# Two transformer layers on one core: the token shift as transfers within SBUF, scores in four banks, and a new order on all engines

## What is computed

```python
def _layer(x, wqkv, qs, ksc, wo, lg, lb, w1, b1, w2, b2):
    h = shift_token(x)                       # the upper half of the channels comes from the token before
    q, k, v = jnp.split(h @ wqkv, 3, axis=-1)
    ...
    q, k = rotary_xpos(l2norm(q) * qs, l2norm(k) * ksc)
    o = local_attention(q, k, v)             # 8 heads of 64, two windows of 128
    x = x + o @ wo
    h = shift_token(x)
    h = (h - mu) / jnp.sqrt(var + 1e-05) * lg + lb
    a, g = jnp.split(h @ w1 + b1, 2, axis=-1)
    return x + (a * gelu(g)) @ w2 + b2
...
x = x + xattn(layernorm(x), ctx)
x = x + layer1(layer0(layernorm(x)))
```

## Time and profile before

| | |
|---|---|
| median of 3 runs (lowest, highest) | 1527.01 us (1526.02, 1528.28) |
| profiled execution | 1526.93 us |
| its span, first to last instruction | 1524.4 us |
| mean granted TensorE clock | 0.981 of 2.4 GHz |
| busy: PE, PE weight load | 1441.3 us (95%), 1277.3 us (84%) |
| busy: DVE (VectorE), ACT (ScalarE), POOL (GpSimd) | 1130.8 us (74%), 938.4 us (62%), 747.1 us (49%) |
| chain that ended last, by engine | PE 75%, DVE 12%, issue 5%, ACT 4%, POOL 2% |

### The profile page before, as it was taken

How to read it: one execution, slowest core, us unless ns; L and a number is a source line. 1 busy time by engine, 2 the same in 40 slices (tenths; PEclk the granted TensorE clock), 3 DMA queues, 4 the chain that set the end, 5 groups by cost and what they waited for, 6 DMA issues and landing times.

```text
span 1524.4 us, 33616 instructions
## 1 busy us (share of the span) xinstructions
PE 1441.3 (95%) x11808; PEld 1277.3 (84%) x11808; DVE 1130.8 (74%) x3102; ACT 938.4 (62%) x2670; POOL 747.1 (49%) x570
## 2 busy tenths in 40 slices
PE   4999999867999999999999899999999999999997
PEld 3888888746889889998888788888888888888886
DVE  3766666456888878887878778878888887888864
ACT  2766666435666666666666667666666666666661
POOL 1121121044666666666555555555565555566642
PEclk8999999889999999999999999999999999999998
DMA  6311111200000000000000110010010001011000
GB/s 196 103 57 48 50 53 44 84 29 15 24 24 24 25 25 23 23 23 24 30 31 24 45 41 24 17 47 31 31 32 31 30 30 30 30 34 40 24 24 26
DMA packets 40843, 58.88 MB, mean 39 GB/s; under 512 B 6540, under 2 KB 22448, under 8 KB 40752
## 3 DMA queue, kind: packets, MB, share of 16 engines
q1 hardware_dynamic: 40752, 57.69, 11.7%
HBM read 38.06 MB, written 16.78 MB: 36 GB/s over the span
## 4 chain that ended last, share of the span: by engine, by line
PE 75%; DVE 12%; issue 5%; ACT 4%; POOL 2%; DMA 1%; SPq 1%; DVEq 0%; POOLq 0%; ACTq 0%
PE pb L511 33%; PE pb L788 7%; PE pb L733 6%; PE pb L802 6%; PE pb L764 5%; PE pb L748 4%; PE pb L826 4%; PE pb L572 2%; PE pb L560 2%; PE pb L610 2%; PE pb L614 2%; DVE p_t L1383 2%; DVE r_cos L1350 2%; DVE p_t L1369 1%; DVE n_sq L1336 1%
## 5 line engine op out<-in xcount | busy, mean ns | idle before, releaser
L1559 POOL TENSOR_TENSOR n_inv<-n_cl,half_neg 128x16 f32<-128x16 f32 x64 | 211.4, 3303 | 190.8 <-DVE n_cl L1341 187.3
L1058 ACT ACTIVATE p_t<-p_t,s_nm 128x128 f32<-128x128 f32 (+1 forms) x512 | 227.2, 448 | 19.5 <-DVE s_nm L1369 18.8
L511 PE MATMUL pb<-h_hi,w_hi 128*128 128x256 f32 x704 | 208.8, 297 | 5.3 <-DVE h_lo L1332 3.3
L511 PE MATMUL pb<-h_lo,w_hi 128*128 128x256 f32 x704 | 199.7, 284 | 0.0
L511 PE MATMUL pb<-h_hi,w_lo 128*128 128x256 f32 x704 | 199.7, 284 | 0.0
L1564 POOL TENSOR_TENSOR r_cos<-r_cos,r_sin 128x1024 f32<-128x1024 f32 x64 | 154.7, 2417 | 88.8 <-DVE r_sin L1356 88.8
L1016 ACT ACTIVATE qk_sq<-pb 128x512 f32<-128x512 f32 x128 | 72.5, 592 | 183.6 <-PE pb L511 183.6
L1049 ACT ACTIVATE pt_t<-pb 128x512 f32<-128x512 f32 x192 | 114.5, 597 | 107.0 <-PE pb L748 106.6
L1369 DVE CUSTOM_DVE_ANT_0 p_t<-pb,mask_t 128x128 f32<-128x128 f32 (+1 forms) x512 | 152.0, 353 | 28.5 <-PE pb L733 27.3
L511 PE MATMUL pb<-wqkv_hi,xt_hi 128*128 128x512 f32 x384 | 166.9, 435 | 5.8 <-DVE r_sin L1356 4.9
L1586 POOL TENSOR_TENSOR hg_lo<-hg,hg_hi 128x256 fp32r<-128x256 f32 x192 | 139.6, 748 | 55.4 <-DVE hg_hi L1400 55.4
(11 more groups left out here) (137 smaller groups left out, 4083.1 us busy)
## 6 DMA issues: line engine op xcount, KB each, us to landing
y_state<-x SPq DMA_DIRECT2D x32, 256.0 KB, 2.0
x_cur<-y_state SPq DMA_DIRECT2D x32, 256.0 KB, 2.7
x_res<-y_state SPq DMA_DIRECT2D x32, 256.0 KB, 2.8
x_in<-x SPq DMA_DIRECT2D x16, 256.0 KB, 2.9
x_state<-x SPq DMA_DIRECT2D x16, 256.0 KB, 2.0
x_orig<-x_state SPq DMA_DIRECT2D x16, 256.0 KB, 2.8
out<-x SPq DMA_DIRECT2D x16, 256.0 KB, 2.2
raw_a<-wqkv SPq DMA_DIRECT2D x2, 1536.0 KB, 8.5
```

The costliest lines, as they stand in the source:

```text
L511: mm = pe.matmul(dst, s, m, start=(n == 0 and k == 0), stop=(n == len(pairs) - 1 and k == 2))
L1058: e = nc.scalar.activation(pu, pu, ACT.Exp, bias=s_nm[:, j, k:k + 1], scale=-1.0, accum_out=s_sum[:, j, k:k + 1])
L1559: nc.gpsimd.tensor_tensor(n_inv[:, t], n_cl[:, t], half_neg[:], ALU.pow).then_inc(pool_inv, 1)
```

## The change

- The shift of x1: TensorE's three products and VectorE's copy are gone; SyncE issues three transfers from SBUF to SBUF (112 rows, 15 rows, one row), and stats_h waits for them. They stand at the head of SyncE's iteration, behind the load of x for the next item; the tail copies of item d come behind them and behind the loads of x_res and x_orig.
- Scores pair 1 goes to banks 5 and 6, so it needs no maxima of pair 0; it waits for x1 (bank 6 has the output product before).
- Turned probabilities have six places. The rotated sine parts have one place in place of two, so rotate waits for the add_parts before it.
- Second bias: in layer 1 it is two rows of the last chunk's weights against rows of ones; the kept rows then are x1 plus the sum of the first phase, and the add L1412 is gone. Layer 0 keeps bias and kept rows as before.
- hidden 5 stands last on TensorE; x_hi waits for the last projection.

The new orders. TensorE: scores 0 and 1, project 0,0, feed 0, project 0,1, feed 1 and 2, project 0,2, scores 2, feed 3, turn_p 0, feed 4 and 5, turn_h, project 1,0 and 1,1, turn_next, turn_p 1, project 1,2, turn_p 2, hidden 0, turn_p 3, hidden 1, turn_p 4, hidden 2, turn_p 5, weigh 0 to 2, hidden 3 and 4, out_product 0, turn_qk 0 to 3, out_product 1, hidden 5.

VectorE: maxes 0, gate_hi 3 of item d, maxes 1 to 3, stats_h, gate_hi 4 and 5, inverse_sums 0, norm_probs 0, inverse_sums 1, rotate 0, inverse_sums 2, norm_h, maxes 4, squares 0, clamp 0, maxes 5, norm_probs 1, inverse_sums 3, second_residual, split_h_hi, norm_probs 2, split_h_lo, norm_probs 3, inverse_sums 4, rotate 1, norm_probs 4, squares 1, gate 0, inverse_sums 5, norm_probs 5, clamp 1, gate 1 and 2, out_lo 0, x_lo, gate 3, gate_hi 0 and 1, gate 4, out_lo 1, gate_hi 2, residual, gate 5.

GpSimd: deviation, gate_lo 3 to 5 of item d, add_parts 0, inverse_norms 0, add_parts 1, inverse_norms 1, norm_qk 0 and 1, kept_rows, gate_lo 0 to 2. ScalarE: the exponentials of units 0 and 1 ahead of the first squares, copies of turned probabilities between the gelus, gelu 5 last.

```diff
+SHIFT_PIECES = [(0, 112), (112, 15)]
...
-        S_BANK = [3, 4, 3, 4, 3, 4]
+        S_BANK = [3, 4, 5, 6, 3, 4]
...
+            def shift_down(c):
+                for first, rows in SHIFT_PIECES:
+                    sp.dma_start(x1[first + 1:first + 1 + rows, :, 1], x1[first:first + rows, :, 2]).then_inc(shift_load, 16)
+                sp.dma_start(x1[0:1, 1, 1], x1[P - 1:P, 0, 2]).then_inc(shift_load, 16)
...
+                if c is not None:
+                    sp.wait_ge(dve_x1, at(c, 1, 1))
+                    shift_down(c)
+                    if b is not None:
+                        sp.dma_start(x_res[:], one(y_dram, seq_of(b, layer))).then_inc(res_load, 16)
...
-            def shift_down(c):
-                pe.wait_ge(dve_x1, at(c, 1, 1))
-                pe.matmul(pb[:, 6, 0:P], down_f, x1[:, 0, 2], start=True, stop=True)
-                pe.matmul(pb[:, 6, P:2 * P], down_f, x1[:, 1, 2], start=True, stop=False)
-                pe.matmul(pb[:, 6, P:2 * P], carry_f, x1[:, 0, 2], start=False, stop=True).then_inc(pe_down, 1)
...
+                elif j == 1:
+                    if c is not None:
+                        pe.wait_ge(dve_x1, at(c, 1, 1))
                 else:
-                    pe.wait_ge(dve_max, at(b, UNITS, 2 * j))
+                    pe.wait_ge(dve_max, at(b, UNITS, 2))
...
-            def copy_shifted(c):
-                dve.wait_ge(pe_down, at(c, 1, 1))
-                nc.vector.tensor_copy(x1[:, :, 1], pb[:, 6, 0:2 * P].rearrange("p (t n) -> p t n", t=NT)).then_inc(dve_down, 1)
-
             def stats_h(c):
-                dve.wait_ge(dve_down, at(c, 1, 1))
+                dve.wait_ge(shift_load, at(c, 48, 48))
...
-                if layer_of(d, layer) == LAYERS - 1:
-                    dve.wait_ge(dve_x2, at(d, 1, 1))
-                    dve.wait_ge(orig_load, at(plus(d, -SEQS), 16, 16))
-                    nc.vector.tensor_tensor(x2[:, par], x2[:, par], x_orig[:], ALU.add).then_inc(dve_out, 1)
...
-            def residual_bias(c, d, layer):
-                ly = layer_of(c, layer)
+            def kept_rows(c, d, layer):
                 pool.wait_ge(dve_x1, at(c, 1, 1))
...
+                if layer_of(c, layer) == LAYERS - 1:
+                    pool.wait_ge(orig_load, at(plus(c, -SEQS), 16, 16))
+                    more = x_orig[:].rearrange("p t (c n) -> p t c n", c=KC)
```

More of the change, by code:

```diff
@@ L473, in run_l @@
                     tail_lo(d)
[L474 to L481, removed]
-                    if layer_of(d, layer) == LAYERS - 1:
[L483 to L490, removed]
+                    sp.wait_ge(dve_x2, at(d, 1, 1))
+                    dst = out_rows if layer_of(d, layer) == LAYERS - 1 else y_dram
+                    sp.dma_start(one(dst, seq_of(d, layer)), x2[:, 1 - par]).then_inc(x2_store[1 - par], 16)
             def between(g):
@@ L498, in _ @@
             l_iterations(sp, run_l, between)
-            sp.wait_ge(x2_store, 16 * ITEMS)
+            for u in range(2):
+                sp.wait_ge(x2_store[u], 8 * ITEMS)
         @block.tensor
@@ L714, in hidden, with scores @@
                 mm.then_inc(pe_w1, 1)
-            def scores(a, b, j):
+            def scores(a, b, c, j):
                 if j == 0:
@@ L832, in run_l @@
                 if b is not None:
[L833 to L837, removed]
+                    scores(a, b, c, 0)
+                    scores(a, b, c, 1)
                 if a is not None:
@@ L875, in run_l @@
                 if b is not None:
+                    turn_p(a, b, d, 3)
+                if c is not None:
+                    hidden(a, b, c, 1)
+                if b is not None:
                     turn_p(a, b, d, 4)
                 if c is not None:
-                    hidden(a, b, c, 1)
                     hidden(a, b, c, 2)
@@ L888, in run_l @@
                     out_product(b, 0)
-                if c is not None:
-                    hidden(a, b, c, 5)
                 if a is not None:
@@ L897, in run_l @@
                     out_product(b, 1)
+                if c is not None:
+                    hidden(a, b, c, 5)
             def between(g):
@@ L1137, in run_l @@
                     next_weights(g, 2)
+                if has_next(a):
+                    x_hi(plus(a, 1))
+                if b is not None:
+                    probs_copy(b, 5)
+                    out_hi(b, 0)
+                if c is not None:
                     gelu(c, 3, layer)
+                if b is not None:
+                    out_hi(b, 1)
+                if c is not None:
                     gelu(c, 4, layer)
-                    gelu(c, 5, layer)
                 if a is not None:
@@ L1145, in run_l @@
                     copy_qk(a, 3)
+                if c is not None:
+                    gelu(c, 5, layer)
             def between(g):
@@ L1475, in run_l @@
                 if c is not None:
-                    gate(c, 0, layer)
-                if b is not None:
-                    out_lo(b, 0)
-                if c is not None:
+                    gate(c, 3, layer)
                     gate_hi(c, 0)
@@ L1492, in run_l @@
                 if c is not None:
-                    gate(c, 5, layer)
-                    gate_hi(c, 3)
-                    gate_hi(c, 4)
-                    gate_hi(c, 5)
+                    gate_hi(c, 2)
                 if b is not None:
                     residual(b)
+                if c is not None:
+                    gate(c, 5, layer)
                 if isinstance(g, int) and g == SEQS - 1:
@@ L1637 @@
     w2 = rows_padded(L0_ffn_w2, FC * P)
-    for copy in (1, 2):
-        w2[:, HID + (copy - 1) * TAIL:HID + copy * TAIL] = w2[:, HID - TAIL:HID]
+    tail = w2[:, HID - TAIL:HID]
+    w2[:, HID:HID + TAIL] = tail
+    w2[:, HID + TAIL + 1:HID + 2 * TAIL + 1] = tail
+    for row in (HID + TAIL, HID + 2 * TAIL + 1):
+        w2[LAYERS - 1, row] = np.asarray(L0_ffn_b2)[LAYERS - 1]
     by_channel = lambda v: np.ascontiguousarray(np.asarray(v).reshape(LAYERS, KC, P).transpose(0, 2, 1))
```

222 lines of the change are left out of this document (121 added, 101 removed).

## The result

The changed kernel takes 1554.47 us (median of 4 runs, 1551.67 to 1555.39) against 1527.64 for the kernel before on the same chip: ratio 1.0173, 95% interval 1.0155 to 1.0191. It is slower by 1.7%; forecast were 1553 and a range of 1504 to 1563. The profiled execution took 1554.36 us.

The account below looks back on a forecast made before the run. TensorE bounds layer 0 before; after the change a ring through VectorE and GpSimd does. Layer 0 +14.9, layer 1 +6.5, weights +2.5 and drain +2, together +26, take 1526.9 to 1553 us; range 1504 to 1563.

Parts of the forecast that it names:

- The period of the ring: Steady iterations of both layers: a ring through VectorE and GpSimd, not TensorE, sets 37.2 us.
- the turn of h: TensorE waits 0.8 us for norm and maxima of unit 4, the norm's second half being held by GpSimd's add.
- the turns of q and k: Near the iteration's end TensorE waits 0.9 us for gate 4, behind casts held by GpSimd's multiply and kept rows.
- GpSimd's power before the two multiplies: Late in GpSimd's queue, 3.3 us, followed without a break by two multiplies of 1.9 each and kept rows of 1.35.
- The steady term: Longer steady iterations: 12 x (37.2-35.96) = +14.9 us in layer 0, 13 x (37.2-36.70) = +6.5 in layer 1.
- Around the weights: Four iterations around the change of weights, 155.28 us before: 0 to +5 us, taken as +2.5.
- the two stalls: TensorE's waits in each iteration: 0.8 us at the turn of h, 0.9 us at the second turn of q and k.
- The drain: After the last full iterations the transfers' landing is exposed: +2 us in all, the removed add set off.
- The transfers: Shift at the head of SyncE's queue lands at 3.7 us, statistics begin at 4.3: no cost, 0.3 to 1.2 us spare.
- Dense TensorE work: TensorE's program without waits takes 35.2 us an iteration, bounds 34.9 and 35.5.
- (a): Rival, chance 0.25: nothing stands still at the norm; 35.6 us an iteration, 1509 us in all, faster.
- (b): Rival, chance 0.13: only the first stall comes, casts slip through; 36.3 to 36.5 us an iteration, 1526 to 1532 in all.

Follow-up runs that it names:

- a1: Changed kernel with one wait more: GpSimd's first add of rotated parts waits until the layer norm is done; 1501.58 us.
- a2: Changed kernel with gate 4 ahead of the casts of chunks 0 and 1 on VectorE; 1543.0 us.
- a6: Changed kernel with GpSimd's first add after the norm, gate 4 before the casts, casts and low parts of chunks 3 to 5 in their own iteration; 1483.3 us.
- after: The changed kernel itself, without further edits, against the kernel before; 1554.47 us, ratio 1.0173.
- a3: Changed kernel with GpSimd's first add after the norm and gate 4 before the casts; casts of chunks 3 to 5 stay in the next iteration; 1498.32 us.
- b2: Kernel before with only the shift as three transfers, issued between the two tail copies; 1519.38 us.
- b1: Kernel before with only layer 1's second bias in the last chunk and the kept rows on GpSimd; 2 us better than its forecast of 1515 to 1519 us.
- a5: Changed kernel with casts and low parts of chunks 3 to 5 back in the iteration of their gates; 1539.95 us.
- a4: Changed kernel with the three shift transfers issued behind the loads of x_res and, in layer 1, x_orig; 1567.16 us.
- b3: Kernel before, in its old order, with both the shift by transfers and the kept rows on GpSimd; 1510.19 us.

## Why the prediction was right, and where its terms were not

The sign, the mechanism of the steady iteration and the time were right; the time was in part luck, since two large errors cancelled. Step by step:

- **The period of the ring.** Forecast 37.2 us in both layers, measured 36.64 and, without the first iteration of layer 1, 36.71. The chain came nearly as written: the norm ended 11.86 us into the iteration (12.0 forecast), TensorE waited 0.76 at the turn of h (0.8), 0.4 in start-to-start time at hidden 1 (0.3), 0.54 around the turns of q and k (0.9); gate 4 ended at 33.0 (33.6). Two of these three waits are shown by removal (a1, a2); hidden 1's wait was not tried by itself, it went with a1. The step that was mis-sized is GpSimd's power before the two multiplies: 3.3 us in the sum, 2.91 in the trace. That is 0.4 of the missing 0.55 us.
- **Why the power was shorter.** In the kernel before, VectorE's product of two SBUF tensors stood over its start; in the new order maxima do. The row from VectorE before, beside the power at 1223.62:

```profile
1223.52 0.69 DVE L1383 TENSOR_TENSOR p_t<-p_t,s_inv 128x512 f32<-128x512 f32 x1
```

  The product ends at 1224.21, and the power takes 0.45 us more than the 2912 ns that all of layer 0 has now. With the norm's small power it is the other way round: 708 ns before, 1231 now, as the first product of probabilities starts just ahead of it (696.85 against 696.87). The traces have no exception: before, 61 of the 64 large powers have such a product over their start and take 3.28 to 3.37 us, the other three 2.91; in the changed kernel none has one, and all 64 take 2.91. Of its 32 small powers 30 have one (1.23), two do not (0.70 and 0.71); in a6 none has, and all take 0.70 to 0.71. That the lost time is a wait at the power's start is read from these rows; no run moved that product alone.
- **The steady term.** 12 x 1.24 and 13 x 0.5 gave +21.4; measured were +8.2 and, without the first iteration of layer 1, 0.0. This term was too large by 13 us.
- **Around the weights.** Forecast +2.5 (0 to +5) for four iterations; measured +8.85, and +3.8 in the next one. The table of parts: of the 164.13 us, the two stalls make 6.0 (after against a3) and the casts' place 4.2 (a3 against a6); without both it is 153.88, under the 155.28 before. The stalls are the forecast's own mechanism, priced there at 0 to 5 us. The casts' place it did not name: it moved the casts of chunks 3 to 5 into the next iteration and then costed only where they stand in a steady one, not that they come behind the splits of weights of 3.1 and 3.3 us there. Most of those 4.2 us are not idle time. The row of a3's four iterations, to set beside that of a6:

```profile
812.26:970.37 158.11, 144.83 (x1146) 131.24 (x1145) 113.30 (x328) 100.41 (x250) 88.26 (x60) 0.96 0.12 37
```

  TensorE idles 13.3 us there against 12.3 in a6, and is busy 144.83 against 141.59 for as many instructions, at a granted clock of 0.96 against 0.99. In a3 the clock stood at the lower of its two levels (1.2 of 2.4 GHz) from 924.3 for 3.4 us, behind a wait of 2.70 us, and from 941.4 for 6.8 us, beginning within a wait of 3.29 us; in a6 only from 854.9 for 3.4 us. No term of the forecast stands for that. That these waits brought the clock down is not shown: a6 has a wait of 2.70 us too, and no lower clock behind it.
- **The first iteration of layer 1.** It took 40.41 us, of which the two stalls make 2.4 (a3: 38.05) and the casts' place 0.7 (a6: 37.37). What is left is 2.9 us above a6's steady 34.51, and there the shift's transfers are late, which the forecast had at no cost. SyncE's queue has the copy of the last chunk's new weights ahead of them, which waits for VectorE's split (L1176, 1002.78 to 1004.52). SyncE, then VectorE, in the changed kernel:

```profile
1004.55 0.63 SPq L454 DMA_DIRECT2D w_hi<-w_lo  x1
1005.22 1.65 SPq L471 DMA_DIRECT2D x<-x  x2
```

```profile
1009.29 0.75 DVE L1320 BATCH_NORM_STATS2 l_st<-x 128x6 f32<-128x256 f32 x2 [1.82 <-DMA x<-x]
```

  The transfers start 3.5 us into the iteration in place of 0.28, and the statistics wait 1.82 us for the landing. In the old order b2, with these transfers, takes 40.21 us there, with a wait of 3.99 us for the landing; b1, without them, 35.91, and the kernel before 36.61. In a6 the statistics still wait 2.0 us; how much of its 2.9 us is the landing and how much the split of 1.74 us on VectorE, no run of the new order parts.
- **The drain.** Forecast +2 for the exposed landing; measured +8.5. The landing is +2.6 (b2), the kept rows -3.5 (b1), and the casts' place +9 (a5 against after; 5.4 as a6 against a3). There TensorE waits 7.0 us for low parts and 4.7 for tail copies; that it has nothing else to do beside an item's last product is read from these waits.
- **The errors cancelled.** The steady term was 13 us too high, weights with the iteration behind them 10 and the drain 6.5 too low. That the total came within 2 us of 1553 is luck; the parts did not earn it.
- **The transfers.** Issued from 0.28 to 2.58, the last landed at 3.6 (3.7 forecast), the statistics began at 4.3 (4.3). In a steady iteration they are free, as costed, and a4 shows that the room is between one load and two; in the first iteration of layer 1 and in the drain they are not.
- **Dense TensorE work** is 34.51 us (a6), not 35.2, and below the bound of 34.9. Added up from start to start in layer 0, the shift's products are 0.59 of the 1.45 us between the kernel before and a6. Scores, turns of probabilities and of x, and the products of the probabilities take another 0.79 less, the wide products 0.08 less. b3, with the old order, stays at 35.3 in its steady iterations, so the gain comes with the new order and its banks; which regrouping gives it, no run shows. In a ring set by VectorE it changed nothing.
- **The rivals.** (a) needed the norm to slip through; it was held in 12 of 12 iterations of layer 0. Forced to do so by a1, the iteration takes 34.91 us, not 35.6, as dense work was overpriced, and the whole 1501.58, not 1509. (b)'s period was 36.3 to 36.5; a2, in which its first stall stays and the last goes, takes 36.12.

**What VectorE and GpSimd do to each other.** In these runs a two-tensor operation, a cast or a TENSOR_SCALAR of VectorE whose operands are all in SBUF stands still beside GpSimd's add, multiply or kept rows: the norm 1433 against 399 ns, the casts near the end, the split of 4.73 against 3.09. The Trainium skill ("SBUF — State Buffer", section "SBUF: two separate sides") says that the shared pair is held for the whole GpSimd instruction; for these the trace agrees: the norm's second half took 2.47 to 2.48 us beside an add of 2.45. For the power on 16 columns it does not: the product at 705.91 lies within the power of 705.03 to 707.94 and takes 0.69 us, and the measurement decides.

## What to carry to other kernels

Before an operation is moved on VectorE, ask which GpSimd instruction will be under way when it starts, and whether its own predecessor is what releases that instruction; one added wait on GpSimd, which starts its add some 0.7 us later, was worth 53 us here (1554.47 to 1501.58). Cost a new order also where the pipeline is not full and where it carries extra work: the casts' place cost 0.2 us in a steady iteration (a3 against a6), 4.2 around the weights, and 5 to 9 in the drain. Where two causes overlap, undo both: undone alone, the casts' place showed 1.1 of its 4.2 us around the weights. And where work moves to a queue, look for what else that queue waits for, in the odd iterations too: one wait for a split of weights made the transfers, free in all steady iterations, 3 us late.

## What was not expected of the hardware

- GpSimd's power on 128x16 takes 2.91 us as long as no product of two SBUF tensors on VectorE stands over its start, and 3.3 with one; on 128x2 it is 0.71 and 1.23. Such products that start inside the large power are not held (64 in the changed kernel, 0.66 to 0.69 us).
- Transfers within SBUF of 112, 15 and 1 rows took 1.65 (the first two together) and 0.61 us to issue, a load of 256 KB into 128 rows 0.33 to 0.43. From issue to landing they took 2.3, 2.1 and 1.7 us (medians). Where nothing covered the landing, this showed: in b2's drain the statistics waited up to 3.7 us for them.
